# Queries and keys as three stacked parts of 32 rows, scaled and rounded by ScalarE, for one single-pass similarity product per half

## The reference, cut to what matters

```
seq_len = x.shape[-2]
normed = _layernorm(x, ln_w, ln_b)
hg = jax.nn.silu(jnp.einsum('bsd,hd->bsh', normed, W_hidden) + b_hidden)
v, gate = jnp.split(hg, 2, axis=-1)
Z = jax.nn.silu(jnp.einsum('bsd,qd->bsq', normed, W_qk) + b_qk)
q = Z * gamma[0] + beta[0]
k = Z * gamma[1] + beta[1]
sim = jnp.einsum('bid,bjd->bij', q, k) / seq_len
A = jnp.square(jax.nn.relu(sim))
V = jnp.einsum('bij,bjd->bid', A, v) * gate
out = jnp.einsum('bih,dh->bid', V, W_out) + b_out
```

## Time and profile before

| | us |
|---|---|
| median of 3 runs | 605.44 |
| lowest and highest | 604.88, 607.84 |
| the profiled execution | 604.04 |
| its span, first to last instruction | 602.3 |
| TensorE matmul busy | 573.0 (95%) |
| VectorE busy | 396.3 (66%) |
| ScalarE busy | 331.8 (55%) |
| GpSimd busy | 275.1 (46%) |

### The profile page before, as it was taken

How to read it: one execution, slowest core, us unless ns; L and a number is a source line. 1 busy time by engine, 2 the same in 40 slices (tenths; PEclk the granted TensorE clock), 3 DMA queues, 4 the chain that set the end, 5 groups by cost and what they waited for, 6 DMA issues and landing times. The chain is left out here.

```text
span 602.3 us, 14356 instructions
## 1 busy us (share of the span) xinstructions
PE 573.0 (95%) x3844; PEld 539.7 (90%) x3845; DVE 396.3 (66%) x1547; ACT 331.8 (55%) x722; POOL 275.1 (46%) x314
## 2 busy tenths in 40 slices
PE   3999999899999999999899999999999999999993
PEld 2898988778888888888799999999999999999993
DVE  4678888766877767778788555555555555555650
ACT  1522323564666776666675555556665555555651
POOL 3323231103656465565466544445555444445533
PEclk9989999998999999999999999999999999999998
DMA  8970000401111121112234333333333333333221
GB/s 288 406 307 1 0 0 2 177 2 41 54 59 59 40 72 46 59 60 68 65 97 94 54 53 53 53 43 48 54 49 50 52 47 52 46 40 40 42 27 21
DMA packets 31832, 42.45 MB, mean 70 GB/s; under 512 B 4596, under 2 KB 27797, under 8 KB 31670
## 3 DMA queue, kind: packets, MB, share of 16 engines
q0 software_dynamic: 13488, 13.74, 14.7%
q1 hardware_dynamic: 18196, 28.16, 14.2%
q10 hardware_dynamic: 114, 0.15, 0.1%
HBM read 24.46 MB, written 17.57 MB: 70 GB/s over the span
## 5 line engine op out<-in xcount | busy, mean ns | idle before, releaser
L808 ACT ACTIVATE hT<-ps,b_i_sb 128x256 f32<-128x256 f32 (+1 forms) x240 | 94.4, 448 | 113.6 <-PE ps L1332 113.5
L1332 PE MATMUL ps<-w_o_sb,hT 128*128 x852 | 145.1, 327 | 0.9 <-ACT hT L808 0.9
L1332 PEld LDWEIGHTS ps<-w_o_sb,hT 128*128 128x128 f32 x852 | 137.6, 191 | 1.3 <-issue 1.3
L694 POOL DMA_INDIRECT out_rows<-const,y_row x71 | 125.6, 1769 | 27.7 <-issue 27.7
L1332 PE MATMUL ps<-n_hi,we_hi 128*128 128x256 f32 (+1 forms) x468 | 124.7, 290 | 1.1 <-DVE we_lo L1213 1.1
L1332 PE MATMUL ps<-n_hi,we_lo 128*128 128x256 f32 (+1 forms) x468 | 92.9, 280 | 0.0
L1332 PEld LDWEIGHTS ps<-n_hi,we_hi 128*128 128x128 f32 x468 | 88.8, 190 | 1.4 <-DVE we_lo L1213 1.4
L1213 DVE TENSOR_TENSOR we_lo<-we_all,we_hi 128x768 fp32r<-128x768 f32 x80 | 73.1, 956 | 14.0 <-issue 13.1
L1332 PEld LDWEIGHTS ps<-n_hi,we_lo 128*128 128x128 f32 x468 | 71.6, 189 | 0.0
L789 ACT ACTIVATE we_hi<-we_all 128x768 fp32r x80 | 63.5, 850 | 3.8 <-DVE tile_expert L1151 2.4
L1332 PE MATMUL ps<-nA_lo,we_hi 128*128 128x256 f32 (+1 forms) x234 | 65.6, 280 | 0.0
(11 more groups left out here) (238 smaller groups left out, 1148.2 us busy)
## 6 DMA issues: line engine op xcount, KB each, us to landing
we_all<-in_w_i SPq DMA_DIRECT2D x8, 768.0 KB, 12.7
conv_only<-lists SPq DMA_DIRECT2D x31, 194.0 KB
w_o_sb<-in_w_o SPq DMA_DIRECT2D x8, 576.0 KB, 18.2
out_rows<-X SPq DMA_DIRECT2D x16, 192.0 KB
X<-in_x SPq DMA_DIRECT2D x1, 1536.0 KB, 10.4
out_rows<-const,y_row POOLq DMA_INDIRECT x71, 3.7
conv_only<-lists SPq DMA_DIRECT2D x9, 97.0 KB
we_all<-in_w_hid SPq DMA_DIRECT2D x1, 776.0 KB, 6.3
```

The costliest lines, as they stand in the source:

```text
L694: pool.indirect_dma_start(out=out, out_offset=bass.IndirectOffsetOnAxis(ap=y_row[:, odd, t:t + 1], axis=0), in_=y_sb[:, odd, t, :], in_off ...
L808: last = act.activation(hT[:, odd, f, 0:n].unsqueeze(1), ps_h[:, b, c, 0:n].unsqueeze(1), ACT.Gelu, bias=b_i_sb[:, ds(e * FCHUNKS + f, 1)])
L1332: return pe.matmul(dst, lhsT, rhs, start=start, stop=stop)
```

## The change

W_qk is stored three times side by side, gamma and beta three times below each other, so that z comes out as three equal groups of 32 rows. ScalarE, right behind the Silu of z, scales z to q and to k with four activations: q in full in the third group of rows (q_full), k in full in the second (k_full), and both rounded to fp32r in all three groups (q_parts, k_parts). It waits for the end of its own Silu first. VectorE then takes, in those single groups, the full number less the rounded one: a subtraction for q and one for k; it waits for ScalarE's activations (qk_hi_done) in place of the Silu (z_done). The 96 rows of q_parts are so high, high, low, those of k_parts high, low, high, and one rounded product over 96 rows gives high x high + high x low + low x high. For each half that is one single-pass matmul. To make room, weighted_b_o of the experts now lies in attnT.

```diff
         def query_key(i):
-            dve.wait_ge(z_done, i + 1)
-            for n, dst in enumerate((qT, kT)):
-                last = dve.tensor_scalar(dst[:, :], zT[:, :], gb_sb[:, n:n + 1], gb_sb[:, 2 + n:3 + n],
-                                         ALU.mult, ALU.add)
+            wait_alone(dve, qk_hi_done, i + 1, ld_const)
+            for parts, full, here in ((q_parts, q_full, Q_LOW), (k_parts, k_full, K_LOW)):
+                last = dve.tensor_tensor(parts[here, :], full[here, :], parts[here, :].bitcast(f32), ALU.subtract)
             last.then_inc(qk_done, 1)
...
+        def query_key_high(i):
+
+            wait_alone(act, z_done, i + 1, ld_const)
+            scales = [(gb_sb[:, n:n + 1], gb_sb[:, 2 + n:3 + n]) for n in range(2)]
+            for full, here, (by, plus) in zip((q_full, k_full), (Q_LOW, K_LOW), scales):
+                act.activation(full[here, :], zT[here, :], ACT.Identity, bias=plus[here, :], scale=by[here, :])
+            for parts, (by, plus) in zip((q_parts, k_parts), scales):
+                last = act.activation(parts[:, :], zT[:, :], ACT.Identity, bias=plus, scale=by)
+            last.then_inc(qk_hi_done, 1)
...
                 act.activation(zT[:, :], ps_z, ACT.Silu).then_inc(z_done, 1)
+                query_key_high(i + 1)
...
-        products(ps_z, w_qk_hi, w_qk_lo, slice(0, QK), False).then_inc(z_ps, 1)
+        products(ps_z, w_qk_hi, w_qk_lo, slice(0, QK3), False).then_inc(z_ps, 1)
...
-            last = mm(ps_sim[:, t, :], kT[:, t * P:(t + 1) * P], qT[:, :])
+            last = mm(ps_sim[:, t, :], k_parts[:, t * P:(t + 1) * P], q_parts[:, :])
...
-        weighted_b_o = sb("weighted_b_o", [P, 2, D])
+        weighted_b_o = attnT[:, :, 0:D]
```

More of the change, by code:

```diff
@@ L37 @@
 QK = 32
+QK3 = 3 * QK
 EXPERTS, FF = 8, 768
@@ L240, in build @@
         mom = sb("mom", [P, HALVES, 2])
-        w_qk_sb = sb("w_qk_sb", [P, 2, QK])
-        w_qk_hi = sb("w_qk_hi", [P, 2, QK], f32r)
-        w_qk_lo = sb("w_qk_lo", [P, 2, QK], f32r)
+        w_qk_sb = sb("w_qk_sb", [P, 2, QK3])
+        w_qk_hi = sb("w_qk_hi", [P, 2, QK3], f32r)
+        w_qk_lo = sb("w_qk_lo", [P, 2, QK3], f32r)
         w_out_sb = sb("w_out_sb", [P, HID // P, OUT_W])
@@ L250, in build @@
         ln_sb = sb("ln_sb", [P, 2, 2])
-        gb_sb = sb("gb_sb", [QK, 4])
+        gb_sb = sb("gb_sb", [QK3, 4])
         b_out_sb = sb("b_out_sb", [P, D])
@@ L266, in build @@
         nB_bias = sb("nB_bias", [KBB, SEQ], f32r)
-        zT, qT, kT = (xc[0:QK, :, :, :].rearrange("p a t c -> p (a t c)")[:, n * SEQ:(n + 1) * SEQ] for n in range(3))
+        zT, q_full, k_full = (xc[0:QK3, :, :, :].rearrange("p a t c -> p (a t c)")[:, n * SEQ:(n + 1) * SEQ]
+                              for n in range(3))
+        Q_LOW, K_LOW = slice(2 * QK, QK3), slice(QK, 2 * QK)
+        q_parts = sb("q_parts", [QK3, SEQ], f32r)
+        k_parts = sb("k_parts", [QK3, SEQ], f32r)
         hT = sb("hT", [P, 2, FCHUNKS, TWO])
@@ L372, in build @@
         ps_nT = ps[:, 0, :].rearrange("p (k n) -> p k n", k=2)
-        ps_z = ps[0:QK, 1, 0:SEQ]
+        ps_z = ps[0:QK3, 1, 0:SEQ]
         ps_sim = ps[:, 1, :].rearrange("p (t n) -> p t n", t=HALVES)
@@ L420, in build @@
             sem(n) for n in ("normed_done", "nT_ps", "nT_done", "z_ps", "z_done", "qk_done"))
+        qk_hi_done = sem("qk_hi_done")
         v_ps, v_done, sim_ps, sim_done, attn_done, gate_ps, gate_done = (
@@ L487, in over_channels, with three_times, one_for_three @@
             return ap.unsqueeze(1).unsqueeze(3).broadcast_to((P, HALVES, GROUPS, GC))
+        def three_times(ap):
+            return ap.rearrange("p (n c) -> p n c", n=3)
+        def one_for_three(ap):
+            return ap.unsqueeze(1).broadcast_to((1, 3, QK))
         def pad_lists(eng, experts, done):
@@ L738, in bias_high_parts @@
                 act.activation(b_hi[lo, 0:HID].bitcast(f32r), ps_b_hid[lo, :], ACT.Copy)
-                act.activation(w_qk_lo[hi, 1, :], ps_b_qk[hi, :], ACT.Copy)
+                act.activation(three_times(w_qk_lo[hi, 1, :]), one_for_three(ps_b_qk[hi, :]), ACT.Copy)
                 act.activation(b_qk_hi[lo, :].bitcast(f32r), ps_b_qk[lo, :], ACT.Copy).then_inc(bias_hi_done, 1)
@@ L1618 @@
     w_i = np.ascontiguousarray(two_parts(L1_ffn_Wi).transpose(2, 0, 1, 3).reshape(P, EXPERTS, 2 * FF))
-    w_qk = np.ascontiguousarray(two_parts(L1_attn_W_qk).swapaxes(0, 1))
+    w_qk = np.ascontiguousarray(np.tile(two_parts(L1_attn_W_qk).swapaxes(0, 1), (1, 1, 3)))
     b_i = np.asarray(L1_ffn_bi).reshape(EXPERTS * FCHUNKS, P)
@@ L1627 @@
         "b_qk": np.asarray(L1_attn_b_qk).reshape(1, -1), "b_i": np.ascontiguousarray(b_i.T),
-        "gamma": np.ascontiguousarray(np.asarray(L1_attn_gamma).T),
-        "beta": np.ascontiguousarray(np.asarray(L1_attn_beta).T),
+        "gamma": np.ascontiguousarray(np.tile(np.asarray(L1_attn_gamma).T, (3, 1))),
+        "beta": np.ascontiguousarray(np.tile(np.asarray(L1_attn_beta).T, (3, 1))),
         "w_out": packed(L1_attn_W_out, P), "w_out_t": packed(np.asarray(L1_attn_W_out).T, KC),
```

5 lines of the change are left out of this document (3 added, 2 removed).

## The result

The changed kernel takes 626.60 us (median of 4 runs, 622.66 to 630.49) against 605.16 us for the kernel before, measured beside it. The ratio is 1.0355, with a 95% interval of 1.0307 to 1.0402: slower by 21.4 us, where 9.5 were forecast. The direction was right, and the forecast size was under half of what came.

What follows compares the result with a forecast made beforehand. TensorE was taken to bound each 10.73 us image, with chain B binding after the change: 4.0 + 14 x 0.3 + 1 = 9.2, rounded +9.5, giving 613.5 us profiled and 615.0 median, range 609 to 621.

Steps and rivals of the forecast that it cites:

- chain B: Loop over two images through ScalarE's row_a, GpSimd, VectorE's u_pow operation and attend: 22.1 us, 11.0 an image, ending last.
- C: Each image's loop: Silu of z, four activations, subtractions, counting, X's addition, l1_done, attend; the forecast gave it no sum.
- Image 0: First image of the attention stage: the square comes 2.1 us later on ScalarE, so attend starts +1.65 us later.
- The tile lists: VectorE's lists in the last two images, 0.95 us above usual before; forecast as much again, +1 (0 to +2).
- GpSimd's link of chain B: From row_a's end through copy, four scattering DMAs and u_pow to the end of b_out's addition: 8.2 us.
- The even images: The eleven images from 2 to 13 of the attention stage, +0.3 us each, +3.3 forecast.
- A: Loop through ScalarE: Silu of z, activations, normalisation, tanh, row_a, Silu of v, square, then attend; 10.3 us an image.
- D: Loop through Silu of z, four activations, normalisation, tanh, rows' weights, l1_done and attend; named in the experiments, without forecast size.
- Rival 1: chain B gives way and A sets 10.3 us an image, about -0.5 us in all: 605 us, chance 0.16.
- The stage start: Images 0 and 1 of the attention stage: +1.65 and +2.35 us, together +4.0 (2.2 with cheap activations).
- Image 1: attend waits for what follows the last four images' scales on VectorE, which start 3.4 us after S, not 1.05: +2.35 us.
- rival 3: TensorE's clock falls to half after the new waits in each image, +24 us: 639 us, chance 0.04.

Runs made afterwards that it cites:

- e8: The kernel before with four ScalarE activations added behind the Silu of z, into a buffer nobody reads; 613.81 us, ratio 1.0146.
- e15: The kernel of e8 with GpSimd's power of u_var issued behind the first scattering DMA; 610.87 us, ratio 1.0108.
- e1: The changed kernel with GpSimd's power of u_var issued behind the first scattering DMA instead of the fourth; 622.71 us, ratio 1.0274.
- e6: The changed kernel with VectorE's counting and slots moved ahead of the two subtractions; 622.47 us, ratio 1.0315.
- e7: The changed kernel with both edits, that of e1 on GpSimd and that of e6 on VectorE; 623.22 us, ratio 1.0292.
- e5: The changed kernel without the two full-precision activations (low parts left out), with GpSimd's order of e1; 609.59 us, ratio 1.0074.
- e9: The kernel of e7 with ScalarE's normalisation moved ahead of the Silu of z; 613.58 us, ratio 1.0125.
- e12: The kernel of e9 with VectorE's scales of the last four images halved, ahead of image 1's low parts and subtractions; 606.77 us, ratio 1.0013.
- e13: The kernel before with the four moves of e12 (GpSimd's power, VectorE's counting and slots, ScalarE's normalisation, the scales of image 1); 605.45 us, ratio 0.9993.
- e4: The kernel before with queries and keys rounded by VectorE and a single-pass similarity over 32 rows, low parts left out; 598.85 us, ratio 0.9881.
- e10: The changed kernel with ScalarE's normalisation moved ahead of the Silu of z as the only edit; 631.73 us, ratio 1.0438.

## Why the prediction was right in direction and short in size

**Which steps failed.** The spans are 26.5 us apart where the sum was 9.5. Of the 17.0 us between them 3.8 are the convolution's and not the change's; 4.5 are in the two images after 13, 4.2 in the eleven even images, 2.6 at the stage start, 1.9 in the last step. That chain B would end last and make the kernel slower was right. Three steps of the sum failed. The loop through the subtractions (C) was named and not summed, and B's own terms were each a little small, so an image takes 11.41 us and not 11.0. Image 0 was put on ScalarE's way through the square, and TensorE waits at another place. The tile lists were taken as "as much again, +1", and not summed along VectorE's path.

**What was right.** TensorE's saving: from the last matmul for v to the second gate it was 1.56 us (199.01 to 200.57) and is 0.68 (212.99 to 213.67), so 0.88 saved, 0.8 to 0.92 forecast. The subtractions: 0.42 us each, 0.43 forecast. GpSimd's link of chain B: 202.90 to 211.08, 8.2 us, 8.2 forecast. B as a mechanism: e8 shows it at 11.08 us an image with VectorE's and TensorE's work as before, and e15 takes it away (10.91 is left).

**The even images: +7.47, +3.3 forecast.** Two things were wrong, one of size and one of reasoning.

The size. The two images from S at 186.45 to S at 209.41 are chain B from end to end, 22.96 us and not 22.1:

```profile
186.45 0.38 ACT L870 ACTIVATE xc<-ps 96x256 f32<-96x256 f32 x1 [2.14 <-PE ps L1358]
...
190.79 0.97 ACT L882 ACTIVATE row_a<-X,u_bias,u_scale 128x192 f32 x2
...
198.93 1.00 POOL L671 TENSOR_TENSOR X<-X,b_out_sb 128x384 f32 x1
...
199.07 0.94 DVE L1217 TENSOR_TENSOR newton<-u_neg,u_pow 128x2 f32<-128x2 f32 x1 [1.74 <-POOL u_pow L666]
...
200.70 0.42 DVE L1092 TENSOR_TENSOR q_parts<-xc,q_parts 32x256 fp32r<-32x256 f32 x1
...
205.37 0.37 DVE L1201 SCALAR_TENSOR_TENSOR from_base<-ps,a_scale,sums 128x8 f32<-128x8 f32 x2 [0.23 <-DVE both_parts L1192]
```

row_a ends at S + 5.31, not + 5.0: the first activation starts 0.49 us after S and not 0.40, and the four take 2.22 (to the next one's start) and not 2.0, since the two on single row groups are 0.61 apart, the other two 0.50. From row_a's end to newton's are 8.25, not 8.2; from there to l1_done 5.73, not 5.5; from l1_done to S 3.67, not 3.4; attend alone now lasts 2.83 in place of 2.76. That is 0.86 us for two images, 0.43 for one, and eleven times that is 4.7, somewhat more than the shortfall of 4.2 here.

The reasoning: the prediction wrote that the subtractions' wait for ScalarE holds up all that VectorE has behind it, and with it attend, but listed only A and B as loops and never summed this one. From its own rows C would have been 0.40 + 2.0 + 0.1 + 0.9 + 3.7 (4.05 with the issue gap) + 0.1 + 3.44, so 10.6 and 11.0 by turns, close to B's 11.0. Measured it is 11.15 and 11.6 by turns (e1), 22.75 for two images, 0.2 under B's 22.96: in the image from 197.60 B ends last, in the next one (S at 209.41) C does, and VectorE coming from newton waits 0.53 us for k_parts. The price of missing C was small for the forecast, since B and C are nearly equal, and large for the advice one would draw from it: e1 removes B and gains 0.09 us an image, e6 shortens C and gains 0.13, e7 does both and stops at D. Rival 1, B giving way, was put at 605; e1 is that case, and 622.7 came, because C and D stand behind B. Among the kernels built on the changed one, only those with all three shortened (e5, e9, e12) come under TensorE's 10.73 of before.

**The stage start: +6.57, +4.0 forecast.** Image 1 was right in mechanism (e12 removes its part) and short in size: attend starts 12.58 us after S, before 9.85, so +2.73 and not +2.35, and the half clock behind the wait lasts longer, so that attend takes 5.36 us for 4.47.

Image 0 was wrong in mechanism. The forecast has attend behind the square, which comes 2.1 us later. In fact TensorE, which went on to the similarity without a wait before, now waits for the subtractions there, and attend, 7.40 us after S and 5.07 before, has no wait of its own. Similarity and attend of image 0 in the changed kernel, and the similarity in e9:

```profile
125.84 0.50 PE L1358 MATMUL ps<-q_parts,k_parts 96*128 96x256 f32 x2 [2.04 <-DVE k_parts L1092]
...
129.42 3.35 PE L1358 MATMUL ps<-attnT,hT 128*128 128x256 f32 x12
```

```profile
121.47 0.50 PE L1368 MATMUL ps<-q_parts,k_parts 96*128 96x256 f32 x2 [2.80 <-DVE k_parts L1097]
```

Behind this wait the clock falls: 0.72 granted over 127 to 133 us, where the kernel before has 1.00 over 119 to 125, and attend lasts 3.35 us for 2.76. So attend starts 2.33 us later and not 1.65, and is longer too. This is also why e9 gained nothing at image 0: the normalisation that it moves is not on this path.

**Images 13 to 15: +6.13, +1.6 forecast.** The tile lists lie on VectorE's path there, as forecast, but the term was guessed from the excess of before and not worked out along a chain. The kernel before shows what it needed. There VectorE's lists lie between the rows' weights and X's addition and take 1.26 us in one image, from the first of these rows to the second, and 2.07 in the next (273.18 to 275.25); only 0.95 of that showed in the time:

```profile
262.35 0.16 DVE L1117 TENSOR_TENSOR n_list<-list_at,const 128x8 f32<-128x8 f32 x1
...
263.61 0.55 DVE L1159 TENSOR_TENSOR X<-X,ps 128x384 f32<-128x384 f32 x1
```

Chain C runs through this very place, so the lists count in full: 2 x 11.15 + 3.33 = 25.6. e1, with B out of the way and the full clock, takes 25.64 us for these two, +3.2. In the changed kernel they take 2.9 us more, and attend alone is 1.35 and 1.68 us longer, so the rest is most likely rival 3, which the forecast gave 0.04. Attend of images 13 and 14 of the changed kernel, and then of e1:

```profile
286.31 4.18 PE L1358 MATMUL ps<-attnT,hT 128*128 128x256 f32 x12 [2.11 <-DVE from_base L1201]
...
300.90 4.51 PE L1358 MATMUL ps<-attnT,hT 128*128 128x256 f32 x12 [1.93 <-DVE from_base L1201]
```

```profile
280.73 2.83 PE L1363 MATMUL ps<-attnT,hT 128*128 128x256 f32 x12 [2.09 <-DVE from_base L1206]
...
293.91 2.83 PE L1363 MATMUL ps<-attnT,hT 128*128 128x256 f32 x12 [1.94 <-issue]
```

The clock granted is 0.83 over 284 to 294 and over 299 to 309 us in the changed kernel, and 1.00 over 278 to 288 and 292 to 302 in e1.

**The last step: +2.53, about +0.6 forecast.** TensorE's first expert product waits 2.75 us for we_lo (VectorE), 1.06 before; VectorE reaches it later. From image 15 to the end the nine kernels built on the changed one take 321.75 to 323.33 us, 322.6 on average, and the seven built on the kernel before 320.11 to 321.85, 321.2 on average; so some 1.4 us of the 2.53 go with the change, and which chain they lie on was not tested.

**Is the change worth anything given room?** With the same four moves in both, e12 needs 10.36 us an image and e13 10.75, 4.2 us for the change over eleven images, and 0.5 at image 1. But image 0 takes 11.34 against 8.31 and images 13 to 15 take 25.36 against 22.22, 6.2 us against it. The medians, 606.77 and 605.45, are not apart by more than such a measurement can tell. e4 shows the other way: a single pass, there without the low parts, is worth 7 us if its operands cost ScalarE nothing.

## What to carry to other kernels

When work is laid on an engine early in a loop, write down every loop through that engine, each consumer of what it now delays, and sum each one in full; the forecast's sentence on VectorE's queue named a loop that then went without a sum. Where two or three loops lie within half a microsecond of each other, each edit alone shows almost nothing (e1, e6), and an edit without gain does not show that the loop which it shortened was off the path. Time saved on the engine that sets the pace is kept only if the price for it is not paid on a loop close behind; here chain B stood 0.8 us an image behind TensorE. Where the order of operations differs, as in the first and last images of a stage, the chain is to be summed again.

## What the runs showed of the hardware

- Waits of the same length met different clocks. TensorE waited 2.11 and 1.93 us in the changed kernel and came back at half speed (attend 4.18 and 4.51 us); it waited 2.09 and 1.94 us at the same places in e1 and kept the full clock (2.83). A wait of about 2 us was followed by a lower clock in some executions here and not in others.
- In the convolution TensorE was busy for the whole of 30 to 40 us, and the clock granted there was 0.50 to 0.99 in different profiles, at a DMA share of 1.02 in each. The end of that stage moves with it, by up to 7.5 us.
- Two activations of 32x256 on different groups of rows (64 to 95, then 32 to 63) started 0.61 us apart and took 1.20 us together; four on the same rows took 2.07 us (e8), 0.50 apart.
- A VectorE operation of 0.15 us on two small tensors lasted 0.88 us beside GpSimd's addition of b_out (newton, 210.23), 1.60 us in e1 (u_bias, to 206.26; that addition ended at 206.23) and 0.45 beside the copy in e10. Each of the three ended within 0.03 us of GpSimd's operation, whether that was the addition or the copy.
